# Feed-forward features as rows read back from device memory, prepared one group earlier, and moments as three split products

## The chip, the cores and the metric

The kernel runs on one core of a Trainium2 chip. The time is device microseconds of one execution, and lower is better. The kernel before took 903.79 us (median of 3 runs, 901.78 to 903.89). The engines are PE (matrix products, with its weight loads as PEld), DVE and ACT (elementwise work, reductions, activations), POOL (elementwise work and masks) and SP, which here only issues transfers.

## The reference, cut to what matters

Sixteen sequences of 256 tokens and 256 channels pass four layers, each with a layer norm and a residual sum: attention with 16 heads, a feed-forward layer, a gated linear attention, and the same feed-forward layer again. The change touches the feed-forward layer, whose weights are made from control points by a cubic spline:

```
def spline_reconstruct(control_points, out_size, in_size):
    n = out_size * in_size
    idx, f = _catmull_rom_grid(control_points.shape[0], n)
    p0, p1, p2, p3 = (control_points[idx[0]], control_points[idx[1]], control_points[idx[2]], control_points[idx[3]])
    ...
    return w.reshape(out_size, in_size)
gate_w = spline_reconstruct(gate_cp, INTER, HIDDEN)      # 1024 x 256
up_w = spline_reconstruct(up_cp, INTER, HIDDEN)
down_w = spline_reconstruct(down_cp, HIDDEN, INTER)
gate = jnp.einsum('bsh,ih->bsi', hidden_states, gate_w)
up = jnp.einsum('bsh,ih->bsi', hidden_states, up_w)
inter = jax.nn.silu(gate) * up
return jnp.einsum('bsi,hi->bsh', inter, down_w)
x = x + _L0_ffn_ref(_layernorm(x, axis=-1), ...)
```

## The kernel before

**Stages.** After the weights are set up the program runs attention (one period for each of the 16 sequences), the first feed-forward stage, the gated stage (periods 0 to 16, the last one a tail) and the second feed-forward stage. `X` holds all tokens on the chip from the first stage to the last.

**A feed-forward stage** has 8 groups g of 512 tokens (two sequences), and each group has 8 steps m of 128 of the 1024 inner channels. The rows of the gate and up weights in one step depend on 42 features of a token only: 14 channels of x, 14 further channels half a row on, and 14 moments, which are products of x with a fixed table `mom`. Each feature is needed as a high part, as the rest (low part) and as the high part again, so one step's gate product has 3 x 42 = 126 rows against `cst` (126 x 128). It is one product of 512 columns, and so is the up product. The down product takes the inner values as a high and a low part and is 12 products of 256 columns.

**How the features come about.** DVE normalises four tiles of 128 tokens into `xr` (L1760). PE turns them (L1001), ACT and DVE copy the turned x into `xf`, and PE multiplies it with the moment table (L1012), in 16 products of 128 columns with plain 32-bit operands. ACT and POOL then spread x and moments into `xe` (L1356, L1369, L640 to L648), tokens on the partitions and 126 features for each step on the free axis. In every step PE turns four 128 x 126 pieces of `xe` (L1022) into `bank_t`, and ACT copies them to `stk` (L1374), which has room for two steps.

**Order of the work.** Each engine runs a list written out by hand, group by group in `period` and step by step inside it, and waits on counting semaphores. In step m PE does the turn for step m + 1, the gate and up products of m (L1048, L1051) and the down product of m - 2 (L396 to L398); ACT does `in_hi` of m - 1 (L1387), the copy to `stk` (L1374) and the SiLU of m (L1379); DVE does `in_lo` of m - 1 (L1778) and the gated product `inter` of m (L1773). `gact`, `inter` and `pair_a`/`pair_b` hold two steps, `in_hi`/`in_lo` four. The features of group g + 1 are made during group g, its statistics during group g - 1. SP stores finished groups in the second feed-forward stage and is otherwise idle in both of them. The down weights `wd_lo` are loaded from device memory in 16 transfers near the end of attention (L513), and the attention's `stack` is filled by transfers from `stage` (L484) to 16 partitions each.

Of the kernel before, what the change touches and what calls it, by code (L numbers as in the profile page):

```python
# [20 lines left out]
ALU = mybir.AluOpType  # L21
# [28 lines left out]
XW = 388  # L50
# [96 lines left out]
def build(nc, x, a_wq, a_wk, a_wv, a_wo, b_wq, b_wk, b_wog, b_wig, g_weight, cpw_in, psi_in, feat_in, mom_in,  # L147
          starts, out):
    outer = ExitStack()
    with outer:  # L150
# [22 lines left out]
        half_neg = sb("half_neg", [P, 2, TB], F32)  # L173
# [18 lines left out]
        mom = sb("mom", [P, CT, MT * KG], F32)  # L192

# [13 lines left out]
        with ExitStack() as at:  # L207
            wq, wk, wv = ((sb(n + "_hi", [P, CT, D], F32R, at), sb(n + "_lo", [P, CT, D], F32R, at))
# [9 lines left out]
            stack = sb("stack", [P, 2, 2, PR, 2, S], F32R, at)  # L218
# [12 lines left out]
        with ExitStack() as ft:  # L231
            xr = sb("xr", [P, 2 * TB, XW], F32, ft)
# [36 lines left out]
        wdx = nc.dram_tensor("wdx", [INTER + 1, D], F32, kind="Internal").ap()  # L269

# [3 lines left out]
        s_cp, s_feat, s_mom = sem("control_points_loaded"), sem("features_loaded"), sem("moment_table_loaded")  # L274
        s_c, s_ch = sem("factors_made"), sem("factors_high")
# [49 lines left out]
        def ffn_semaphores():  # L325
# [8 lines left out]
            f.bn, f.mv, f.ve, f.xn, f.xc = own("bn", 4), own("mv", 4), own("ve", 1), own("xn", 4), own("xc", 1)  # L334
            f.up, f.il, f.res = own("up", MT), own("il", MT), own("res", 2)
            f.dve = [f.bn, f.mv, f.ve, f.xn, f.xc, f.up, f.il, f.res]
            f.rs, f.xl, f.ml = own("rs", 1), own("xl", 1), own("ml", 1)
            f.pool = [f.rs, f.xl, f.ml]

            f.xh, f.xa, f.mo, f.mh = own("xh", 1), own("xa", 1), own("mo", 1), own("mh", 1)  # L340
            f.st, f.si, f.ih = own("st", MT), own("si", MT), own("ih", MT)
            f.act = [f.xh, f.xa, f.mo, f.mh, f.st, f.si, f.ih]

            f.xT, f.mp, f.tp = own("xT", 2), own("mp", 1), own("tp", MT)
            f.gp, f.upp, f.dp = own("gp", MT), own("upp", MT), own("dp", MT + 1)
            f.pe = [f.xT, f.mp, f.tp, f.gp, f.upp, f.dp]
# [70 lines left out]
        def run_pairs(period):  # L417

            def run(eng):
                period(0, 0, prev=False)  # L420
                with eng.Fori(0, PAIRS // 2 - 2) as j:
                    period(2 * j + 1, 1)
                    period(2 * j + 2, 0)
                period(PAIRS - 3, 1)
                period(PAIRS - 2, 0, nxt2=False)
                period(PAIRS - 1, 1, nxt=False, nxt2=False)
            return run
# [13 lines left out]

        def gathered(b):

            at = b * (P + 1) + 2
            return xr[:, :, at:at + P].rearrange("p t (m s) -> p t m s", s=KG)[:, :, :, 0:NB]

        def spread(u, copy, b):

            return xe[:, u, :, :, copy, NB * b:NB * b + NB]
# [9 lines left out]
        def _(sp):  # L459
# [9 lines left out]
            lead(sp, a_stk + a_md)  # L469
# [61 lines left out]

            run_periods(sp, period)
            sp.wait_ge(a_res, upto(a_res, B - 1, 1))
# [3 lines left out]
            with sp.Fori(0, PAIRS - 1) as g:  # L537
                sp.wait_ge(f_.res, upto(f_.res, g + PAIRS, 2))
                sp.dma_start(out_t[:, bass.ds(2 * TB * g, 2 * TB), :],
                             X[:, bass.ds(2 * TB * g, 2 * TB), :]).then_inc(s_out, 16)  # L540
# [8 lines left out]
        def _(pool):  # L549
# [6 lines left out]
            pool.memset(half_neg[:, :, :], -0.5).then_inc(s_const, 1)  # L556
# [10 lines left out]
            pool.tensor_copy(ident16[:, :], ident[:, :]).then_inc(s_const, 1)  # L567

            def rstd(b, u):
                pool.wait_ge(a_ve, upto(a_ve, b, 1))  # L570
                pool.tensor_tensor(rs[:, u, :], ve[:, u, :], half_neg[:, 0, :], ALU.pow).then_inc(a_rs, 1)
# [40 lines left out]
            def period(b, j, u, prev=True, nxt=True, nxt2=True, nxt3=True):  # L612
                for p in range(NP):
# [3 lines left out]
                    if nxt and not nxt2:  # L617
# [1341 lines left out]
```

## Time and profile before

| | before |
|---|---|
| median of 3 runs | 903.79 us |
| the profiled execution: its time, its span | 903.31 us, 901.6 us |
| busy: PE, PEld, DVE, ACT, POOL | 829.0, 707.9, 642.2, 541.2, 324.7 us |
| granted TensorE clock, mean | 0.973 |
| first gate product of the first feed-forward stage | 383.37 us |
| first gate product of the second feed-forward stage | 715.08 us |

The profiled execution takes 1.7 us more than its span; that lies outside the first and the last instruction. A busy PE need not be at its peak, since the ends of pipelined products are modelled: what one costs is read from the distance between starts. A granted clock of 1.00 is 2.4 GHz, 0.50 is 1.2 GHz. The DMA share is the mean busy share of 16 transfer engines.

### The profile page before, as it was taken

To read this page: it belongs to the slowest core of one execution; us is meant where nothing else is said; L and a number is where in the kernel's file an instruction comes from. 1 tells how busy PE (TensorE), PEld (TensorE's weight loads), DVE (VectorE), ACT (ScalarE), POOL (GpSimd) and SP (SyncE) were. 2 spreads that over 40 slices of the span, in tenths; PEclk is the share of its full clock that TensorE was granted. 3 is DMA by queue.
4 is the path that set the end of the run, shared out by engine and by line. 5 is a ranking of instruction groups with operands and counts; after the bars stand their busy time and mean duration, and the time that the engine had idled before them with its cause. 6 is when DMAs were issued, how large, how long until landed. Compare 5 with 4: busy or idle time off the path is not lost.

```text
span 901.6 us, 21452 instructions
## 1 busy us (share of the span) xinstructions
PE 829.0 (92%) x7348; PEld 707.9 (79%) x7348; DVE 642.2 (71%) x1287; ACT 541.2 (60%) x1062; POOL 324.7 (36%) x386
## 2 busy tenths in 40 slices
PE   3599899999999997689999999899999799999998
PEld 3477677777777775578888888799998688888887
DVE  7566777777778776457766766688888666667765
ACT  2146445545554554466666667598887566666664
POOL 3932223222322224233323331057666733333320
PEclk9779999999999999799999999999999899999999
DMA  5955666765676562000000000000000000000001
GB/s 178 119 82 85 132 94 97 97 93 83 100 96 88 87 89 49 7 17 1 1 0 0 1 1 1 1 1 0 0 0 1 1 1 25 24 23 23 24 25 47
DMA packets 33767, 40.54 MB, mean 45 GB/s; under 512 B 4335, under 2 KB 25232, under 8 KB 33664
## 3 DMA queue, kind: packets, MB, share of 16 engines
q1 hardware_dynamic: 33706, 39.74, 26.9%
q8 instruction: 36, 0.59, 0.3%
q14 instruction: 25, 0.20, 0.1%
HBM read 8.79 MB, written 5.24 MB: 16 GB/s over the span
## 4 chain that ended last, share of the span: by engine, by line
PE 51%; DVE 16%; ACT 13%; issue 9%; POOL 4%; SPq 3%; DMA 2%; DVEq 1%; ACTq 1%; POOLq 0%
PE bank L396 7%; PE bank L397 6%; PE bank L398 6%; DVE inter L1773 5%; PE pair_a L815 4%; ACT gact L1379 4%; ACT stk L1374 4%; PE bank L829 4%; PE pair_b L784 3%; PE bank L1012 3%; PE pair_b L1138 2%; PE bank L1022 2%; DVE in_lo L1778 2%; DVE st L1747 2%; PE bank L1138 2%
## 5 line engine op out<-in xcount | busy, mean ns | idle before, releaser
L577 POOL TENSOR_SCALAR_AFFINE_SELECT prob<-prob 128x512 f32<-128x512 f32 x128 | 82.3, 643 | 210.0 <-ACT prob L1250 210.0
L396 PE MATMUL bank<-wd_hi,in_hi 128*128 128x256 f32 x512 | 147.7, 288 | 8.5 <-DVE X L1784 6.8
L1778 DVE TENSOR_TENSOR in_lo<-inter,in_hi 128x512 fp32r<-128x512 f32 x128 | 97.7, 763 | 77.9 <-ACT in_hi L1387 77.3
L1250 ACT ACTIVATE prob<-pair_a 128x768 f32<-128x768 f32 x128 | 103.7, 810 | 74.3 <-PE pair_a L815 73.2
L398 PE MATMUL bank<-wd_hi,in_lo 128*128 128x256 f32 x512 | 142.9, 279 | 0.0
L397 PE MATMUL bank<-wd_lo,in_hi 128*128 128x256 f32 x512 | 142.8, 279 | 0.0
L1387 ACT ACTIVATE in_hi<-inter 128x512 fp32r<-128x512 f32 x128 | 80.9, 632 | 94.7 <-DVE inter L1773 94.6
L1618 DVE TENSOR_REDUCE mx<-pair_b 128x6 f32<-128x768 f32 x124 | 118.1, 952 | 26.2 <-PE pair_b L796 25.2
L1773 DVE TENSOR_TENSOR inter<-gact,pair_b 128x512 f32<-128x512 f32 x128 | 87.6, 685 | 36.8 <-ACT gact L1379 36.3
L396 PEld LDWEIGHTS bank<-wd_hi,in_hi 128*128 128x128 f32 x512 | 97.1, 190 | 16.4 <-issue 6.0
L397 PEld LDWEIGHTS bank<-wd_lo,in_hi 128*128 128x128 f32 x512 | 97.5, 190 | 3.6
L398 PEld LDWEIGHTS bank<-wd_hi,in_lo 128*128 128x128 f32 x512 | 96.8, 189 | 0.0
L1022 PE MATMUL bank<-ident,xe 128*126 128x128 f32 x512 | 81.0, 282 | 9.4 <-ACT stk L1374 5.3
L1374 ACT ACTIVATE stk<-bank 126x512 fp32r<-126x512 f32 x128 | 75.2, 587 | 12.8 <-PE bank L1022 12.6
L815 PE MATMUL pair_a<-stack 50*128 50x256 f32 x512 | 66.1, 336 | 14.4 <-DMA stack<-mrow 9.3
L1379 ACT ACTIVATE gact<-pair_a 128x512 f32<-128x512 f32 x128 | 75.9, 593 | 0.0
L1022 PEld LDWEIGHTS bank<-ident,xe 128*126 128x126 f32 x512 | 58.1, 142 | 18.5 <-ACT stk L1374 12.7
L640 POOL COPY xe<-xr 128x448 f32<-128x448 f32 x32 | 24.7, 773 | 130.9 <-ACT xe L1356 130.9
L815 PEld LDWEIGHTS pair_a<-stack 50*128 50x128 f32 x512 | 39.4, 189 | 39.6 <-issue 15.8
L784 PE MATMUL pair_b<-stack 48*128 48x256 f32 x496 | 55.9, 303 | 7.2 <-DVE stage L1609 3.6
L1048 PE MATMUL pair_a<-stk,cst 126*128 126x512 f32 x128 | 62.3, 487 | 0.0
L1238 ACT ACTIVATE stage<-bank 128x512 fp32r<-128x512 f32 x32 | 19.2, 599 | 57.0 <-PE bank L398 52.3
(222 smaller groups left out, 2132.2 us busy)
## 6 DMA issues: line engine op xcount, KB each, us to landing
stack<-stage SPq DMA_DIRECT2D x192, 128.0 KB, 4.7
X<-in_attn_a_x SPq DMA_DIRECT2D x14, 256.0 KB, 5.0
result<-X SPq DMA_DIRECT2D x7, 512.0 KB, 2.9
stack<-mrow SPq DMA_DIRECT2D x128, 4.0 KB
wdx<-spline SPq DMA_DIRECT2D x1, 1024.0 KB
wd_lo<-wdx SPq DMA_DIRECT2D x16, 64.0 KB
spline<-factor_basis SPq DMA_DIRECT2D x1, 1008.0 KB, 6.5
X<-in_attn_a_x SPq DMA_DIRECT2D x1, 512.0 KB, 7.5
```

The source lines that it names most:

```text
L396: pe.matmul(dst, l_hi, r_hi, start=first, stop=False)
L397: pe.matmul(dst, l_hi, r_lo, start=False, stop=False)
L398: return pe.matmul(dst, l_lo, r_hi, start=False, stop=last)
L784: pe.matmul(dst[:, n, at_col:at_col + S], stack[rows, u, h, p % PR, 0, P * t:P * t + P], stack[rows, u, h, p % PR, 1, :], start=(t == 1), ...
L815: i = pe.matmul(pair_a[:, n, at_col:at_col + S], stack[rows, u, h, p % PR, 1, P * t:P * t + P], stack[rows, u, h, p % PR, 0, :], start=Tru ...
L1022: i = pe.transpose(bank_t[0:NFX, P * t:P * t + P], xe[:, u, t, m].rearrange("p c f -> p (c f)").bitcast(F32), ident[:, :])
L1250: act.activation(prob[:, p % 4], pair_a[:, :, P:4 * P], ACT.Exp, scale=DK ** -0.5).then_inc(a_e, 1)
L1374: act.activation(stk[:, m % 2, :], bank_t[0:NFX, :], ACT.Copy).then_inc(f_.st, 1)
L1379: act.activation(gact[:, m % 2, :], pair_a[:, m % 2, :], ACT.Silu).then_inc(f_.si, 1)
L1618: dve.tensor_reduce(mx[:, h, :, p % PR, :], src[:, :, 0:3 * P].rearrange("p n (t k) -> p n t k", t=3), AX.X, ALU.max).then_inc(a_mx, 1)
L1773: dve.tensor_tensor(inter[:, m % 2, :], gact[:, m % 2, :], pair_b[:, m % 2, :], ALU.mult).then_inc(f_.up, 1)
L1778: dve.tensor_tensor(in_lo[:, m % LAG, :], inter[:, m % 2, :], in_hi[:, m % LAG, :].bitcast(F32), ALU.subtract).then_inc(f_.il, 1)
```

## The change

`xe`, its spreading on ACT and POOL, the turns of its pieces on PE and the copies to `stk` are gone. ACT now normalises x into `xr`, PE turns it, ACT and DVE split the turned x into a high part and a low part (`fs`), and PE multiplies both parts with a split moment table in 6 products of 512 columns, whose result ACT and DVE split as well. SP writes `fs` to a table `fx` in device memory, in 3 transfers of 128 x 2 x 512 values, one row for each channel or moment. It then reads back, in 9 transfers of 14 x 8 x 512 values, the 14 rows of each kind for all 8 steps: for the high, the low and the high part again. `stk` holds all 8 steps of two groups. There is one `fx`, so the rows of the next group are written only when the reads of the group before have landed (`f_.ld`), and read only when they have been written (`f_.fw`). Features of group g + 2 are made during group g, their statistics during group g - 1. Features of the first two groups are made at the end of attention and of the gated stage.

On SP, in the loop of a feed-forward stage; `X` is the residual, `result` the output. Before, only the second stage has such a loop:

```order
L539 ISA [waits f_res]
L539 DMA result<-X 128x4x256
L537 REGISTER_ALU
L537 COMPARE_AND_BRANCH
L544 DMA result<-X 128x2x256 [waits f_res] x2
```

Now, for one group in the second stage (the first has the same without `result`):

```order
L555 ISA [waits f_fw]
L561 DMA stk<-fx 14x8x512 [waits f_upp]
L561 DMA stk<-fx 14x8x512 x8
L575 ISA
L576 ISA [waits f_res]
L576 DMA result<-X 128x4x256
L541 ISA
L542 ISA [waits f_xl]
L544 DMA fx<-fs 128x2x512 [waits f_ld]
L544 DMA fx<-fs 128x2x512
L548 REGISTER_ALU
L550 DMA fx<-fs 128x2x512 [waits f_ml]
```

Reads of one group, the store and the writes of the next group take turns, with a wait between reads and writes on either side.

On PE, step 6 of a group before (the 12 down products of a step begin with the last row shown):

```order
L1022 MATMUL bank<-ident,xe 126x128 [waits f_st]
L1022 MATMUL bank<-ident,xe 126x128 x3
L1048 MATMUL pair_a<-stk,cst 128x512 [waits f_si,f_st]
L1051 MATMUL pair_b<-stk,cst 128x512 [waits f_up]
L396 MATMUL bank<-wd_hi,in_hi 128x256 [waits f_il]
```

Now, step 5, the one with the moments of group g + 2 (`fs`, `mom_hi`, `mom_lo`):

```order
L1071 MATMUL pair_a<-stk,cst 128x512 [waits f_si]
L1074 MATMUL pair_b<-stk,cst 128x512 [waits f_up]
L412 MATMUL bank<-fs,mom_hi 128x512 [waits f_xl,moment_table_low]
L413 MATMUL bank<-fs,mom_hi 128x512
L414 MATMUL bank<-fs,mom_lo 128x512
L412 MATMUL bank<-fs,mom_hi 128x512
L413 MATMUL bank<-fs,mom_hi 128x512
L414 MATMUL bank<-fs,mom_lo 128x512
L412 MATMUL bank<-wd_hi,in_hi 128x256 [waits f_il]
```

The turns and the wait for `f_st` are gone from every step. A group's first gate product waits for `f_ld`, its own 9 reads.

The diff, cut (8 leading blanks of each line are left out):

```diff
-XW = 388
+FSTEP = P + 1
+FROWS = 3 * FSTEP + 5
...
-    xf = sb("xf", [P, CT, 2 * S], F32, ft)
-    stk = sb("stk", [NFX, 2, 2 * S], F32R, ft)
-    xe = sb("xe", [P, 2, 2 * TB, MT, 3, NF], F32R, ft)
+    stk = sb("stk", [P, 2, MT, 2 * S], F32R, ft)
+    xr = sb("xr", [P, 2 * TB, D], F32, ft)
+    fs = sb("fs", [P, 2, 3, 2 * S], F32R, ft)
...
+fx = nc.dram_tensor("fx", [2, FROWS, 2 * S], F32, kind="Internal").ap()
...
+        def write_x(g):
+            sp.wait_ge(f_.xl, upto(f_.xl, base + g, CT))
+            sp.wait_ge(f_.ld, upto(f_.ld, base + g - 1, 144))
+            for c in range(CT):
+                sp.dma_start(fx[:, P * c:P * c + P, :].rearrange("v p t -> p v t"),
+                             fs[:, :, c, :].bitcast(F32)).then_inc(f_.fw, 16)
+        def write_moments(g):
+            sp.wait_ge(f_.ml, upto(f_.ml, base + g, 1))
+            at = 2 + 2 * FSTEP
+            sp.dma_start(fx[:, at:at + P, :].rearrange("v p t -> p v t"),
+                         fs[:, :, CT, :].bitcast(F32)).then_inc(f_.fw, 16)
+        def read(g, u):
+            sp.wait_ge(f_.fw, upto(f_.fw, base + g, 48))
+            sp.wait_ge(f_.upp, upto(f_.upp, base + g - 2, MT))
+            for n, part in enumerate((0, 1, 0)):
+                for r in range(3):
+                    rows = fx[part, 2 + FSTEP * r:2 + FSTEP * r + P, :]
+                    rows = rows.rearrange("(m s) t -> s m t", s=KG)[0:NB]
+                    at = NF * n + NB * r
+                    sp.dma_start(stk[at:at + NB, u].bitcast(F32), rows).then_inc(f_.ld, 16)
+        def period(g, u, prev=True, nxt=True, nxt2=True, nxt3=True):
+            if nxt:
+                read(g + 1, 1 - u)
+            if prev:
+                store(g - 1)
+            if nxt2:
+                write_x(g + 2)
+                write_moments(g + 2)
+        return write_x, write_moments, read, run_pairs(period)
...
+    sp.wait_ge(s_zero, 1)
+    sp.dma_start(fx[:, D, :].rearrange("v (p k) -> v p k", k=32), zeros[:, :]).then_inc(s_zeros, 16)
+    f1_write_x(0)
+    f1_write_moments(0)
+    sp.wait_ge(a_stp, upto(a_stp, B - 2, NP))
+    sp.wait_ge(s_zeros, 16)
+    f1_read(0, 0)
+    f1_write_x(1)
+    f1_write_moments(1)
     sp.wait_ge(a_res, upto(a_res, B - 1, 1))
...
                  ).then_inc(s_gload, 16)
     sp.dma_start(win[:, :, :], starts).then_inc(s_gload, 16)
-    with sp.Fori(0, PAIRS - 1) as g:
...
+        def period(g, u, prev=True, nxt=True, nxt2=True, nxt3=True):
+            if nxt3:
+                rstd4(g + 3)
...
-            pe.wait_ge(s_mom, 16)
-            pe.wait_ge(f_.xa, upto(f_.xa, base + g, 1))
-            pe.wait_ge(f_.xc, upto(f_.xc, base + g, 1))
-            for t in range(2 * TB):
-                for c in range(CT):
-                    i = pe.matmul(dst[:, P * t:P * t + P], xf[:, c, P * t:P * t + P], mom[:, c, :],
-                                  start=c == 0, stop=c == CT - 1)
+            pe.wait_ge(s_moml, 1)
+            pe.wait_ge(f_.xl, upto(f_.xl, base + g, CT))
+            for c in range(CT):
+                i = mm3(pe, dst[:, :], mom_hi[:, c, :], mom_lo[:, c, :], fs[:, 0, c, :], fs[:, 1, c, :],
+                        c == 0, c == CT - 1)
             i.then_inc(f_.mp, 1)
-        def turn_rows(g, u, m):
-            pe.wait_ge(f_.st, upto(f_.st, base + g, m))
-            if m == 0:
-                pe.wait_ge(f_.ml, upto(f_.ml, base + g, 1))
-            for t in range(2 * TB):
-                i = pe.transpose(bank_t[0:NFX, P * t:P * t + P],
-                                 xe[:, u, t, m].rearrange("p c f -> p (c f)").bitcast(F32), ident[:, :])
-            i.then_inc(f_.tp, 1)
         def down(g, m):
...
-        def period(g, u, prev=True, nxt=True, nxt2=True):
+        def period(g, u, prev=True, nxt=True, nxt2=True, nxt3=True):
             for m in range(MT):
-                if m < MT - 1:
-                    turn_rows(g, u, m + 1)
-                elif nxt:
-                    turn_rows(g + 1, 1 - u, 0)
-                pe.wait_ge(f_.st, upto(f_.st, base + g, m + 1))
+                if m == 0:
+                    pe.wait_ge(f_.ld, upto(f_.ld, base + g, 144))
                 pe.wait_ge(f_.si, upto(f_.si, base + g, m - 1))
-                pe.matmul(pair_a[:, m % 2, :], cst[:, 0, m, :], stk[:, m % 2, :], start=True,
+                pe.matmul(pair_a[:, m % 2, :], cst[:, 0, m, :], stk[0:NFX, u, m, :], start=True,
                           stop=True).then_inc(f_.gp, 1)
                 pe.wait_ge(f_.up, upto(f_.up, base + g, m - 1))
-                pe.matmul(pair_b[:, m % 2, :], cst[:, 1, m, :], stk[:, m % 2, :], start=True,
+                pe.matmul(pair_b[:, m % 2, :], cst[:, 1, m, :], stk[0:NFX, u, m, :], start=True,
                           stop=True).then_inc(f_.upp, 1)
-                if m in (2, 3) and nxt:
-                    if m == 2:
-                        pe.wait_ge(f_.mh, upto(f_.mh, base + g, 1))
-                    else:
-                        pe.wait_ge(f_.xa, upto(f_.xa, base + g + 1, 1))
-                    turn_in(g + 1, 1 - u, m - 2, bank_p)
-                if m == 4 and nxt:
-                    moments(g + 1, bank_p)
+                if m == 2 and nxt2:
+                    pe.wait_ge(f_.ml, upto(f_.ml, base + g + 1, 1))
+                    turn_in(g + 2, 0, bank_t)
...
+        def normalise4(g):
+            act.wait_ge(f_.mr, upto(f_.mr, base + g, 1))
+            act.wait_ge(f_.xT, upto(f_.xT, base + g - 1, CT))
+            act.sem_inc(passed_act, 1)
+            for t in range(2 * TB):
+                act.activation(xr[:, t, :], X[:, bass.ds(2 * TB * g + t, 1), :], ACT.Identity,
+                               bias=fnmr[:, t:t + 1], scale=frs[:, t:t + 1]).then_inc(f_.xn, 1)
+        def high_x(g, c, src):
+            act.wait_ge(f_.xT, upto(f_.xT, base + g, c + 1))
+            act.wait_ge(f_.fw, upto(f_.fw, base + g - 1, 48))
+            act.activation(fs[:, 0, c, :], src[:, :], ACT.Copy).then_inc(f_.xh, 1)
+        def high_moments(g, src):
             act.wait_ge(f_.mp, upto(f_.mp, base + g, 1))
-            act.activation(xr[:, :, D + 4:XW], src[:, :].rearrange("p (t k) -> p t k", t=2 * TB),
...
                     high_inner(g if m else g - 1, (m - 1) % MT)
-                if m < MT - 1:
-                    rows(g, m + 1)
-                elif nxt:
-                    rows(g + 1, 0)
                 silu(g, m)
-                if nxt:
+                if nxt2:
+                    if m == 0:
+                        normalise4(g + 2)
                     if m == 2:
-                        high_x(g + 1, 1 - u)
-                        store_turned(g + 1, bank_p)
-                    if m == 4:
-                        high_moments(g + 1, 1 - u, bank_p)
+                        high_x(g + 2, 0, bank_t)
+                        high_x(g + 2, 1, bank_p)
+                    if m == 5:
+                        high_moments(g + 2, bank_t)
...
+        def low_x(g, c, src):
+            dve.wait_ge(f_.xh, upto(f_.xh, base + g, c + 1))
+            dve.tensor_tensor(fs[:, 1, c, :], src[:, :], fs[:, 0, c, :].bitcast(F32),
+                              ALU.subtract).then_inc(f_.xl, 1)
+        def low_moments(g, src):
+            dve.wait_ge(f_.mh, upto(f_.mh, base + g, 1))
+            dve.tensor_tensor(fs[:, 1, CT, :], src[:, :], fs[:, 0, CT, :].bitcast(F32),
+                              ALU.subtract).then_inc(f_.ml, 1)
...
-                    stats4(g + 2)
-                if m == 3 and nxt:
-                    store_turned(g + 1, bank_p)
+                if nxt3:
+                    if m < 2:
+                        stats2(g + 3, m)
+                    if m == 1:
+                        mean_rest(g + 3)
+                if nxt2:
+                    if m == 2:
+                        low_x(g + 2, 0, bank_t)
+                    if m == 3:
+                        low_x(g + 2, 1, bank_p)
+                    if m == 5:
...
                 g_products(n)
             if nxt:
                 g_values(n + 1, 1 - u)
+            if at == B - 3:
+                pe.wait_ge(g_.xl, upto(g_.xl, B - 1, 1))
+                f2_turn(0, 0, bank_t)
+            if at == B - 2:
+                f2_moments(0, bank_t)
             if not prev:
                 g_turn(n + 2, u)
```

## Rows read from the trace of the kernel before

**Rows 1.** Windows view, one stretch of the first feed-forward stage; its columns are the first row.

```profile
core 0: us, PE busy (x) PEld busy (x) DVE busy (x) ACT busy (x) POOL busy (x), PEclk, DMA share, GB/s
430.00:453.00 23.00, 22.40 (x171) 20.14 (x170) 16.19 (x33) 15.19 (x29) 7.13 (x7) 1.00 0.01 1
```

**Rows 2.** Timeline of PE: start, us, engine, line, operation, output<-inputs, count, [idle<-releaser].

```profile
452.67 0.47 PE L1048 MATMUL pair_a<-stk,cst 126*128 126x512 f32 x1
...
454.47 0.28 PE L398 MATMUL bank<-wd_hi,in_lo 128*128 128x256 f32 x1
454.75 0.65 PE L1022 MATMUL bank<-ident,xe 128*126 128x128 f32 x4
455.17 0.48 PE L1048 MATMUL pair_a<-stk,cst 126*128 126x512 f32 x1
...
464.91 2.02 PE L1012 MATMUL bank<-mom,xf 128*128 128x128 f32 x16 [0.21 <-DVE xf L1767]
466.69 0.36 PE L396 MATMUL bank<-wd_hi,in_hi 128*128 128x256 f32 x1
```

**Rows 3.** Timeline of ACT in the same stretch.

```profile
453.58 0.63 ACT L1387 ACTIVATE in_hi<-inter 128x512 fp32r<-128x512 f32 x1 [0.89 <-DVE inter L1773]
454.12 0.58 ACT L1374 ACTIVATE stk<-bank 126x512 fp32r<-126x512 f32 x1
454.60 0.59 ACT L1379 ACTIVATE gact<-pair_a 128x512 f32<-128x512 f32 x1
```

**Rows 4.** Timeline of DVE in the same stretch.

```profile
455.38 0.69 DVE L1773 TENSOR_TENSOR inter<-gact,pair_b 128x512 f32<-128x512 f32 x1 [0.43 <-ACT gact L1379]
...
458.48 1.28 DVE L1784 TENSOR_TENSOR X<-bank,X 128x512 f32 x2
...
470.61 1.40 DVE L1747 BATCH_NORM_STATS2 st<-X 128x6 f32 x4
...
472.58 0.17 DVE L1754 TENSOR_SCALAR ve<-mv 128x4 f32<-128x4 f32 x1
```

**Rows 5.** Timeline of PE: first gate products of both stages' first and last group.

```profile
383.37 0.47 PE L1048 MATMUL pair_a<-stk,cst 126*128 126x512 f32 x1
...
545.87 0.48 PE L1048 MATMUL pair_a<-stk,cst 126*128 126x512 f32 x1
...
715.08 0.77 PE L1048 MATMUL pair_a<-stk,cst 126*128 126x512 f32 x1
...
876.11 0.48 PE L1048 MATMUL pair_a<-stk,cst 126*128 126x512 f32 x1
```

**Rows 6.** Timeline of SP's queue, then windows view, while `wd_lo` is loaded.

```profile
349.63 6.04 SPq L513 DMA_DIRECT2D wd_lo<-wdx  x16
356.00:357.00 1.00, 0.84 (x17) 0.47 (x17) 0.00 (x0) 1.00 (x2) 0.23 (x2) 1.00 0.59 88
```

**Rows 7.** Windows view, stack loads queued.

```profile
28.00:30.00 2.00, 0.00 (x0) 0.00 (x0) 0.00 (x0) 0.39 (x1) 1.83 (x2) 1.00 1.06 118
```

**Rows 8.** The page's DMA issues (us to landing), and windows view of one store.

```profile
result<-X SPq DMA_DIRECT2D x7, 512.0 KB, 2.9
770.50:771.00 0.50, 0.50 (x3) 0.10 (x1) 0.00 (x0) 0.50 (x2) 0.34 (x1) 1.00 1.02 346
```

**Rows 9.** One line of the program (L534, load of `gw_row`): its landing.

```profile
DMA to landing us min/median/max: 3.0/3.0/3.0
```

**Rows 10.** Timeline of PE and windows view behind an idle stretch.

```profile
363.92 0.80 PE L815 MATMUL pair_a<-stack 50*128 50x256 f32 x4 [4.78 <-DMA stack<-mrow]
364.00:366.00 2.00, 2.00 (x20) 1.01 (x20) 1.65 (x5) 1.57 (x3) 0.28 (x1) 0.50 0.01 4
```

**Rows 11.** Timeline of ACT in the last attention period.

```profile
363.21 0.63 ACT L1298 ACTIVATE wd_hi<-wd_lo 128x512 fp32r<-128x512 f32 x1 [3.88 <-DMA wd_lo<-wdx]
```

**Rows 12.** Timeline of PE at the end of the gated stage.

```profile
699.05 2.75 PE L1138 MATMUL pair_b<-val,spline 128*128 128x256 f32 x12
...
712.71 0.91 PE L1022 MATMUL bank<-ident,xe 128*126 128x128 f32 x4 [3.11 <-POOL xe L648]
```

More of the change, by code:

```diff
@@ L1071, in run @@
                     down(PAIRS - 1, MT - 1)
-                return turn_in, moments, turn_rows, run
+                return turn_in, moments, run
             def g_turn(n, u, dst=bank_t):
@@ L1321, in period @@
                         spread_rows(2 * p + 1)
+                    if isinstance(b, int) and b == 1 and p == 4:
+                        act.wait_ge(s_mom, 16)
+                        act.activation(mom_hi[:, :, :], mom[:, :, :], ACT.Copy).then_inc(s_momh, 1)
+                    if nxt and not nxt2 and p == 7:
+                        f1_normalise(0)
                     if not nxt:
-                        if p == 0:
-                            act.wait_ge(s_gc, 1)
-                            f1_high_x(0, 0)
+                        if p in (1, 5):
+                            for c in range(CT):
+                                f1_high_x(p // 4, c, pair_b[:, c, :])
                         if p == 2:
-                            f1_store_turned(0, pair_b[:, 0, :])
-                        if p in (3, 4, 5, 7):
-                            high_down(min(p - 3, 3))
-                        if p == 6:
-                            f1_high_moments(0, 0, pair_b[:, 0, :])
+                            f1_normalise(1)
+                        if p in (3, 7):
+                            f1_high_moments(p // 4, pair_b[:, 0, :])
+                        if p in (2, 4, 6, 7):
+                            high_down((p - 1) // 2)
                     if p == 0:
@@ L1411, in run @@
                     high_inner(PAIRS - 1, MT - 1)
-                return high_x, store_turned, high_moments, rows, run
+                return normalise4, high_x, high_moments, run
             def g_high_turned(n, u, src=bank_t):
@@ L1499, in period @@
                         g_normalise(n - 2, u)
-                    if cur and not nxt:
-                        f2_high_x(0, 0)
-                        f2_store_turned(0, bank_t)
-                    if not cur:
-                        f2_high_moments(0, 0, bank_t)
+                    at = n if isinstance(n, int) else None
+                    if at == B - 2:
+                        f2_high_x(0, 0, bank_t)
+                    if at == B - 1:
+                        f2_high_moments(0, bank_t)
+                        f2_normalise(1)
+                    if at == B:
+                        f2_high_x(1, 1, bank_p)
                     if nxt2 and prev:
                         g_norm(n + 2, u)
+                    if at == B - 3:
+                        f2_normalise(0)
                     if prev:
@@ L1548, in _ @@
             copy_att(B - 1)
-            f1_rows(0, 0)
             run_f1()
```

310 lines of the change are left out of this document (156 added, 154 removed).

## The prediction

> **What bounds the kernel now.** I read the windows view first, one group of a feed-forward stage. PE is busy for 22.40 of 23.00 us at a granted clock of 1.00, DVE for 16.19, ACT for 15.19, POOL for 7.13, and the transfers move 1 GB/s [rows 1]. So these stages wait for PE, and the transfer engines stand idle. The distance between first and last group gives the period: (545.87 - 383.37) / 7 = 23.2 us in the first stage, (876.11 - 715.08) / 7 = 23.0 in the second [rows 5]. Inside a group the timeline of PE comes next. A step without moments takes 455.17 - 452.67 = 2.50 us. Its last down product starts at 454.47 and the turns at 454.75. A product of 256 columns takes about 0.12 at full clock, so PE stands for about 0.16 us before the turns, and the turns take 455.17 - 454.75 = 0.42 [rows 2]. Behind PE runs a loop of ACT and DVE that is nearly as long as the step: `in_hi`, the copy to `stk`, SiLU (0.59), then the gated product on DVE (0.69), which releases the next `in_hi` [rows 3, 4].
>
> **What goes.** PE loses 8 x (0.42 + 0.16) = 4.6 us a group. That leaves 1.92 us for a step (the gate product at 452.67 to the last down product's end), 8 x 1.92 = 15.4 for a group. The turns of x stay: two of 0.42 and about 0.2 of waits, 1.0. The moments took 466.69 - 464.91 = 1.78 us in 16 products [rows 2]; 6 products of 512 columns at some 0.23 (twice the 0.12) are 1.4. PE then needs 15.4 + 1.0 + 1.4 = 17.8 us. ACT loses the copy to `stk`, 454.60 - 454.12 = 0.48 us, out of the loop, which falls from 2.50 to about 2.02, 8 x 2.02 = 16.2 us [rows 3]. POOL's spreading lies beside other work and goes at no gain, but for the wait of 3.11 us before the second stage [rows 12].
>
> **What comes on ACT and DVE.** DVE's statistics are cut in two halves in steps 0 and 1. In step 1 stand half of four statistics, the operations on means (0.17 each, four or five of them) and the residual sum of two products at 1.28 [rows 4]: 0.7 + 0.7 + 1.3 = 2.7 us beside the gated product and `in_lo`, which leave some 0.9 of a step free. That costs about 1.8 us a group, between 0 (if the two-step buffers catch it) and 2.7. Normalising on ACT adds four tiles, of which I take 0.5 us onto the loop, and the bound is 0 to 1.6. The feature work ends there: 16.2 + 1.8 + 0.5, with the wait at the moments, is 19.3 us where PE needs 17.8. If nothing else bound the group, it would lose 3.8 us.
>
> **What comes on SP, and takes the bound.** There is one `fx`, and its writes and reads exclude each other. Reads of g + 1 wait for its three writes; writes of g + 2 wait for those nine reads. A group starts when its reads have landed. So a group can't be shorter than T = R + W, reads plus writes with their latencies, whatever the engines do.
> W: three writes of 512 KB. Such a store has landed 2.9 us after its issue, and the transfers move 346 GB/s meanwhile [rows 8]. The two others add 524 KB / 346 = 1.5 each: W = 2.9 + 3.0 = 5.9 us.
> R: 9 transfers of 14 x 8 x 2 KB are 2.064 MB. The fixed part comes from a load of 128 KB that lands after 3.0 us [rows 9]: less its own transfer it is some 1.6 us, or up to 2.6. The rate of loads to 14 partitions isn't in the trace. Near rows are loads to 8 partitions at 88 GB/s on a share of 0.59 of 16 engines, 9.3 GB/s for a busy engine (11 if only 8 carried them) [rows 6]; loads to 16 partitions from on-chip memory at 118 GB/s, 7.4 an engine [rows 7]; and stores at 346 GB/s, 21.6 an engine [rows 8]. If 14 engines serve 14 partitions, these make 130, 154, 103 and 303 GB/s. I take 132, the loads from device memory by their share: 15.7 us, R = 17.3, with ends at 8.4 (303 GB/s) and 21.6 (103).
> T = 17.3 + 5.9 = 23.2 us: by chance the period of before. PE would be idle for T - 17.8, some 5 us at each group's start.
>
> The Trainium skill has a rule for such transfers ("SBUF — State Buffer", section "Door 1: The DMA port swizzle"): the bandwidth goes by how many of 16 ports the partitions reach, four partitions in a row share one, and four ports give about 109 GB/s. Fourteen partitions in a row reach four. The trace is a little above it for 16 partitions (118) and well above it for 8, where two ports would be 54 GB/s and the row shows 88 [rows 6, 7]; I go by the rows from device memory. By the page's figure the sum would be some 966 us, an estimate. That is close to the third rival, which the rows give by themselves.
>
> **The clock.** Behind an idle stretch of 4.78 us PE runs at a granted clock of 0.50 for the next two microseconds at least [rows 10]; a gate product then takes 0.77 in place of 0.48 [rows 5]. With PE idle for 5 us in every group, several microseconds run at 0.50 in each: 17.8 + 4 = 22 us from the group's start, the end of the group's work. It still fits in 23.2, as the reads don't wait for it.
>
> **The sum**, against the profiled execution of 903.31 us (0.5 below the median):
> Entry of the first stage: in the last attention period ACT waits for `wd_lo` until 363.21 [rows 11], and the split of group 0's moments stands behind that. Three us of work and 2.9 of landing make 369.2; + 17.3 = 386.5 for the first gate product, against 383.37 [rows 5]: +3.1.
> Seven periods: 7 x (23.2 - 23.2) = 0. The last group has no reads behind it and runs at compute's pace, -3.8, but starts after idle at half clock, +3; with the wait for its reads I take +1.5 in all, bounds -3 and +4.
> Entry of the second stage: group 0's moments come in period 14 of the gated stage, behind the products at 699.05 [rows 12]. They are split and written at about 705.9; + 17.3 = 723.2 against 715.08: +8.1. The 3.11 us of POOL's wait are gone but inside this.
> Seven periods: 7 x (23.2 - 23.0) = +1.4. Stores of 512 KB share the engines with the reads, six at 0.3, +1.8. Last group: +1.
> Sum: 3.1 + 0 + 1.5 + 8.1 + 1.4 + 1.8 + 1 = +16.9, so **920 us**. R stands in it 16 times (14 periods, two entries): each microsecond of R is 16 us of time. The forecast is no change where R is 16.2, or 141 GB/s. A fixed part between 1.2 and 2.8 us puts the case at 905 to 944.
>
> **Rivals.** *Reads at 11 GB/s an engine (not slower).* For it: the share of 0.59 counts waits in the queue as busy, and 8 engines would carry 8 partitions. 154 GB/s gives R = 13.4 + 1.6 = 15.0, T = 20.9, 2.3 less, 16 x 2.3 = 37 off the forecast: 883 us. It decides from 141 GB/s up. Against it: idle PE for 3 us in each group, whose half clock comes back as compute that lasts as long as T.
> *The engines set the pace.* If the rate goes by engine as in stores, T is 14.3 and the engines' 19.3 bounds: 7 x (19.3 - 23.2) + 7 x (19.3 - 23.0) = -53, entries and ends -1: 849 us. This is what the change does if transfers are hidden; it needs 178 GB/s or more. For it: 21.6 GB/s is what one engine has been seen to carry [rows 8]. Against it: no row of a load to few partitions comes near.
> *Reads like the stack's.* 103 GB/s gives R = 21.6, T = 27.5, 16 x 4.3 = 69 more: 989 us. For it: the same size of tile, the same count of partitions. Against it: those loads also read from on-chip memory.
> *The two effects cancel* by chance, within 0.3% (900.6 to 906.0), about what a measurement of this kernel can tell from no change.
>
> **Chances.** Forecast (905 to 944) 0.37, 11 GB/s an engine 0.25, engines set the pace 0.14, like the stack 0.18, the rest between them 0.06. Faster by over 0.3%: 0.25 + 0.14 + 0.02 = 0.41; within: 0.04; slower: 0.37 + 0.18 = 0.55. The range takes in all of the second, nearly all of the third and the lower part of the fourth (by 16 us for each of R, up to R = 20.5): 848 to 972.
>
> **What would show it.** In the trace after: each group's first gate product idle for about 5 us with the transfer to `stk` as its releaser; first gates 23.2 us apart, and not 19.3, 20.9 or 27.5; the nine reads landing some 17 us behind the first one's issue and the writes within 6; mean traffic of (2.06 + 1.57 MB) / 23.2 us = 157 GB/s; first gates at about 386.5 and 723; a granted clock of 0.50 at group starts; a step of ACT and DVE of about 2.0 us without `stk`. The prediction is wrong if first gates don't wait for transfers at all (R below 13.4), or if the reads move at another rate than 132 GB/s; the period then tells which. It is wrong too if steps of PE stay at 2.5 us, since then the turns weren't what a step costs.

## The result, and the profile after

The changed kernel takes 969.96 us (median of 4 runs, 962.88 to 972.51), the kernel before 903.15 us (with a fourth run beside the three listed above): a ratio of 1.0729, with an interval of 1.0666 to 1.0793, slower. The forecast was 920. The profiled execution has a span of 970.5 us, 68.9 more than before. Medians here leave out a slow execution, one over 1.5% above the fastest of the same kernel; there is one, among the ten of e2.

The page of the kernel after: a summary by engine, the group of the gate product (busy us, mean ns | idle us before it and what ended it), the chain of what ended last, and two DMA issues.

```profile
span 970.5 us, 19870 instructions
PE 803.6 (83%) x6676; PEld 684.8 (71%) x6676; DVE 632.1 (65%) x1272; ACT 502.4 (52%) x967; POOL 237.2 (24%) x306
...
PE 41%; DMA 37%; SPq 9%; DVE 5%; issue 3%; POOL 3%; ACT 3%; ACTq 0%; POOLq 0%; DVEq 0%
...
L1071 PE MATMUL pair_a<-stk,cst 126*128 126x512 f32 x128 | 59.9, 468 | 102.1 <-DMA stk<-fx 102.1
...
fx<-fs SPq DMA_DIRECT2D x48, 512.0 KB, 4.0
...
result<-X SPq DMA_DIRECT2D x7, 512.0 KB, 17.0
```

PE works 25 us less than before and is idle 102.1 us in front of the first gate product of a group, each time until `stk<-fx` has landed. DMA has 37% of the chain, where it had 2%.

Gate products that end such a wait, in the timeline of PE of the kernel after (the first, second and last group of the first stage, and of the second):

```profile
396.28 0.77 PE L1071 MATMUL pair_a<-stk,cst 126*128 126x512 f32 x1 [6.13 <-DMA stk<-fx]
421.32 0.79 PE L1071 MATMUL pair_a<-stk,cst 126*128 126x512 f32 x1 [5.88 <-DMA stk<-fx]
...
581.00 0.79 PE L1071 MATMUL pair_a<-stk,cst 126*128 126x512 f32 x1 [10.03 <-DMA stk<-fx]
...
764.92 0.77 PE L1071 MATMUL pair_a<-stk,cst 126*128 126x512 f32 x1 [7.28 <-DMA stk<-fx]
790.07 0.49 PE L1071 MATMUL pair_a<-stk,cst 126*128 126x512 f32 x1 [3.57 <-DMA stk<-fx]
...
945.89 0.79 PE L1071 MATMUL pair_a<-stk,cst 126*128 126x512 f32 x1 [8.67 <-DMA stk<-fx]
```

The period is (581.00 - 396.28) / 7 = 26.4 us, and (945.89 - 764.92) / 7 = 25.9 in the second stage. Before it was 22.9 and 23.0, and not 23.2 and 23.0 as the prediction had it. The row at 545.87 in [rows 5] isn't the first gate product of the last group but its second: a stage has 64 gate products, eight for each group, and the 57th starts at 543.58. Timeline of PE before:

```profile
543.58 0.48 PE L1048 MATMUL pair_a<-stk,cst 126*128 126x512 f32 x1
545.87 0.48 PE L1048 MATMUL pair_a<-stk,cst 126*128 126x512 f32 x1
```

So the period before is (543.58 - 383.37) / 7 = 22.9 us. SP's queue in the kernel after shows what the period is made of. A row is a run of issues with its start and its length.

```profile
474.27 0.89 SPq L544 DMA_DIRECT2D fx<-fs  x2
475.32 0.77 SPq L550 DMA_DIRECT2D fx<-fs  x1
479.94 3.83 SPq L561 DMA_DIRECT2D stk<-fx  x9
500.62 0.90 SPq L544 DMA_DIRECT2D fx<-fs  x2
501.64 0.81 SPq L550 DMA_DIRECT2D fx<-fs  x1
506.28 3.82 SPq L561 DMA_DIRECT2D stk<-fx  x9
527.24 0.90 SPq L544 DMA_DIRECT2D fx<-fs  x2
```

Writes are issued as soon as the reads have landed, and the next reads as soon as the writes have: W = 479.94 - 474.27 = 5.7 and 506.28 - 500.62 = 5.7 us, R = 500.62 - 479.94 = 20.7 and 527.24 - 506.28 = 21.0. Over the seven groups of the stage R is 20.1 on the mean (18.0 to 21.1) and W 6.3 (5.7 to 7.4). The windows view of the kernel after, inside the reads of another group (columns as in [rows 1]):

```profile
457.00:465.00 8.00, 8.00 (x58) 7.48 (x57) 6.51 (x10) 4.54 (x9) 0.00 (x0) 1.00 0.94 112
432.00:440.00 8.00, 8.00 (x58) 7.47 (x56) 6.47 (x10) 4.46 (x8) 0.00 (x0) 1.00 0.94 129
```

The transfer engines are busy for 0.94 of the time and move only 112 GB/s. The second row is inside the reads of the group before, the shortest ones of the stage (R = 446.50 - 428.52 = 18.0): there the same transfers ran at 129. So 112 is the usual rate and not a fixed one; nothing here shows why that group's was higher.

### The profile page after: what moved, and what is told of

Its sections match the earlier page's. It is cut to its first block, busy times and chain, and to the rows that moved or that the text cites. A ratio compares the mean times of both kernels' runs of the same rounds, so it can differ in the third digit from the quotient of the medians.

```text
span 970.5 us, 19870 instructions
## 1 busy us (share of the span) xinstructions
PE 803.6 (83%) x6676; PEld 684.8 (71%) x6676; DVE 632.1 (65%) x1272; ACT 502.4 (52%) x967; POOL 237.2 (24%) x306
## 2 busy tenths in 40 slices
DMA packets 64997, 98.67 MB, mean 102 GB/s; under 512 B 7153, under 2 KB 28050, under 8 KB 64898
## 4 chain that ended last, share of the span: by engine, by line
PE 41%; DMA 37%; SPq 9%; DVE 5%; issue 3%; POOL 3%; ACT 3%; ACTq 0%; POOLq 0%; DVEq 0%
DMA stk<-fx 27%; DMA fx<-fs 8%; PE bank L412 6%; SPq L561 5%; PE bank L413 4%; PE bank L414 4%; PE pair_a L850 4%; PE bank L864 3%; PE pair_b L819 3%; PE pair_b L1159 2%; PE bank L1159 2%; PE pair_a L1124 1%; POOL spline L649 1%; PE pair_b L831 1%; PE bank L868 1%
## 5 line engine op out<-in xcount | busy, mean ns | idle before, releaser
L413 PE MATMUL bank<-wd_lo,in_hi 128*128 128x256 f32 x512 | 153.7, 300 | 0.0
L414 PE MATMUL bank<-wd_hi,in_lo 128*128 128x256 f32 x512 | 153.7, 300 | 0.0
L1071 PE MATMUL pair_a<-stk,cst 126*128 126x512 f32 x128 | 59.9, 468 | 102.1 <-DMA stk<-fx 102.1
L1825 DVE TENSOR_TENSOR in_lo<-inter,in_hi 128x512 fp32r<-128x512 f32 x128 | 89.0, 696 | 63.4 <-ACT in_hi L1415 62.6
L412 PEld LDWEIGHTS bank<-wd_hi,in_hi 128*128 128x128 f32 x512 | 107.5, 210 | 18.1 <-DVE X L1831 6.0
L413 PEld LDWEIGHTS bank<-wd_lo,in_hi 128*128 128x128 f32 x512 | 106.9, 209 | 5.7
L414 PEld LDWEIGHTS bank<-wd_hi,in_lo 128*128 128x128 f32 x512 | 106.4, 208 | 0.0
L1071 PEld LDWEIGHTS pair_a<-stk,cst 126*128 126x128 f32 x128 | 27.9, 218 | 106.1 <-issue 63.4
L689 POOL TENSOR_TENSOR frs<-fve,half_neg 128x4 f32<-128x4 f32 x16 | 17.2, 1076 | 209.5 <-DVE fve L1799 209.5
L1074 PE MATMUL pair_b<-stk,cst 126*128 126x512 f32 x128 | 57.0, 445 | 0.0
L819 PEld LDWEIGHTS pair_b<-stack 48*128 48x128 f32 x496 | 40.0, 194 | 14.3 <-DVE mx L1653 7.6
L1268 ACT ACTIVATE stage<-bank 128x512 fp32r<-128x512 f32 x32 | 19.1, 597 | 56.8 <-PE bank L414 52.0
```

Source lines behind the costliest of these rows:

```text
L412: pe.matmul(dst, l_hi, r_hi, start=first, stop=False)
L413: pe.matmul(dst, l_hi, r_lo, start=False, stop=False)
L414: return pe.matmul(dst, l_lo, r_hi, start=False, stop=last)
L819: pe.matmul(dst[:, n, at_col:at_col + S], stack[rows, u, h, p % PR, 0, P * t:P * t + P], stack[rows, u, h, p % PR, 1, :], start=(t == 1), ...
L1071: pe.matmul(pair_a[:, m % 2, :], cst[:, 0, m, :], stk[0:NFX, u, m, :], start=True, stop=True).then_inc(f_.gp, 1)
L1825: dve.tensor_tensor(in_lo[:, m % LAG, :], inter[:, m % 2, :], in_hi[:, m % LAG, :].bitcast(F32), ALU.subtract).then_inc(f_.il, 1)
```

## The experiments

My theory after the result (P): the rate of 112 GB/s is set by where the rows land, 14 neighbouring partitions of the on-chip memory. The rival (Q): it is the price of a 2 KB packet from device memory on each transfer engine. Beside it stood three more questions: whether the chain of reads and writes really holds the group, what pace the engines keep without it, and what mutual exclusion costs.

**e1: rows 9 partitions apart.** The read and the order of factor rows to match it:

```diff
-at = NF * n + NB * r
-sp.dma_start(stk[at:at + NB, u].bitcast(F32), rows).then_inc(f_.ld, 16)
+at = 3 * n + r
+sp.dma_start(stk[at:at + 9 * NB - 8:9, u].bitcast(F32), rows).then_inc(f_.ld, 16)
-cx = sb("cx", [P, 2, MT, 3, NF], F32R, at)
+cx = sb("cx", [P, 2, MT, NB, 9], F32R, at)
```

Expected: 

> The changed kernel with one thing different: the 14 rows of a read land on partitions 9 apart (0, 9, ... 117 and so on) in place of 14 neighbours, and the factors' rows are stored in the same new order, so the product is the same. Bytes, packets, transfers and engines used are the same. Theory P (the rate is set by how far the 14 partitions of one transfer lie apart): reads go from 112 to some 200 to 300 GB/s, R from 20 to 9-12 us, the engines' 19.3 us bounds a group, total 850 to 870 us. Theory Q (each engine takes some 270 ns for a 2 KB packet from device memory, wherever it lands): R stays 20 us, groups 26.1 us, total 965 to 975 us.

Measured: 862.92 us (862.04 to 864.62), a ratio to the kernel before of 0.9547 (0.9514 to 0.958), and 107 us below the changed kernel. SP's queue, the windows view inside reads, and PE's timeline in e1:

```profile
406.74 7.46 SPq L561 DMA_DIRECT2D stk<-fx  x9
417.78 0.88 SPq L544 DMA_DIRECT2D fx<-fs  x2
```

```profile
409.00:415.00 6.00, 3.72 (x29) 3.35 (x28) 5.06 (x15) 2.94 (x6) 1.21 (x2) 0.97 0.77 252
```

```profile
455.89 0.39 PE L412 MATMUL bank<-wd_hi,in_hi 128*128 128x256 f32 x1 [2.12 <-DVE X L1837]
```

Same bytes, packets (64997 in the whole trace, as in the changed kernel) and rows in device memory: R is at most 417.78 - 406.74 = 11.0 us and the rate 252 GB/s (227 to 245 in windows of 8 us inside the reads of five groups). Q falls. No gate product waits for `stk<-fx` now; the one long wait left in a group is for DVE's residual sum.

**e2 and e3: fewer bytes.** From the third group of a stage on, three of nine reads (e2) or all nine (e3) bring one step of eight:

```diff
+first = isinstance(g, int) and g < 2
+steps = 1 if n in (2,) and not first else MT      # e3: n in (0, 1, 2)
-rows = rows.rearrange("(m s) t -> s m t", s=KG)[0:NB]
+rows = rows.rearrange("(m s) t -> s m t", s=KG)[0:NB, 0:steps]
```

Expected of e2: 

> The changed kernel, but from the third group of each stage on the three reads of the second high copy bring only the first of eight steps (the other steps keep older values, so this part of the computation is left out). Bytes of a group's reads fall from 2.06 to 1.46 MB. Chain theory (a group lasts reads plus writes): at 112 GB/s R is 13.0 + 1.6 = 14.6, a group 20.3 us, 12 groups lose 5.8 each, 70 in all: 900 us. Rival (something else holds the group at 26, the reads only end beside it): within 10 us of 970.

Expected of e3: 

> As before, with all nine reads cut to one of eight steps from the third group of each stage on (the values of the other steps are old ones): reads are then 0.26 MB a group. The transfer chain would be some 11 us a group, so this shows the pace of the engines alone. My estimate of 19.3 us gives 12 x 6.8 = 82 less, 888 us. Rival: the engines' own pace is worse than worked out (DVE crowd, normalising on ACT, moments), 21 to 22 us: 908 to 920 us. If it is PE alone (17.8): 870.

Measured: 908.46 us (901.97 to 914.01) and 887.51 us (880.9 to 889.03). The last gates of the first stage in both (PE timeline, e2 first):

```profile
525.51 0.50 PE L1073 MATMUL pair_a<-stk,cst 126*128 126x512 f32 x1 [1.61 <-DMA stk<-fx]
546.58 0.80 PE L1073 MATMUL pair_a<-stk,cst 126*128 126x512 f32 x1 [5.01 <-DMA stk<-fx]
```

```profile
424.06 0.79 PE L1073 MATMUL pair_a<-stk,cst 126*128 126x512 f32 x1 [6.20 <-DMA stk<-fx]
```

In e2 the wait for `stk<-fx` stands in front of every short group of the stage but one, and their period is 20.7 us (5 periods; 21.1 in the second stage), where the chain was worked out at 20.3: with three tenths less to read it still ends last. The total is 8 us above the 900 expected, and far from the rival's 960 to 980. In e3 the row shown is the last such wait of that stage, the second group's; from the third on no gate product waits, and groups follow each other at 19.0 and 19.2 us (5 periods of either stage). So 19.1 us is the engines' own pace on the mean, where I had worked out 19.3. Part of that agreement is luck: the last two of the five periods have no statistics in them, and the last one no features either (18.2 and 15.6 to 16.0 us), which the 19.3 didn't allow for. The three full ones take 19.7 to 21.4 us, 20.5 on the mean.

**e4: two tables.** Writes of a group wait for the reads of the last but one:

```diff
-fx = nc.dram_tensor("fx", [2, FROWS, 2 * S], ...)
+fx = nc.dram_tensor("fx", [2, 2, FROWS, 2 * S], ...)
-sp.wait_ge(f_.ld, upto(f_.ld, base + g - 1, 144))
+sp.wait_ge(f_.ld[v], upto(f_.ld[v], base + g - 2, 144 - 72 * v))
```

Expected: 

> The changed kernel with two tables in device memory, one for even and one for odd groups, so that the writes of a group no longer wait for the reads of the group before; all is still issued by SP in the same order. Chain theory: the writes stand behind the reads in the queue and the next reads wait for the writes, so that only the latency between reads and writes goes, some 1.5 to 2 us a group: 24.3 us a group, 942 to 950 us. Rival (mutual exclusion is what costs, transfers of both kinds would overlap): the group falls to the reads alone, 20 us, total 885 us.

Measured: 951.53 us (948.6 to 955.3). SP's queue in e4:

```profile
495.21 3.83 SPq L561 DMA_DIRECT2D stk<-fx  x9
503.40 0.90 SPq L544 DMA_DIRECT2D fx<-fs  x2
507.56 0.36 SPq L550 DMA_DIRECT2D fx<-fs  x1
520.35 3.82 SPq L561 DMA_DIRECT2D stk<-fx  x9
```

The writes are issued 8.2 us after the reads, in the middle of them, but the next reads start no earlier than 25.1 us after the last ones, for the bytes queue. The mean period is 24.3 us in the first stage, as expected; the total is just above the 942 to 950, and far from the rival's 885. Exclusion costs the latency between the two, some 2 us a group; the bytes cost the rest.

**e5 and e6: other spacings.** Eight of nine reads with a step of 2 and of 8 partitions, one execution each (the factors keep their old order, so rows and factors don't match; the time is what is read):

```diff
+k = 3 * n + r
+at = k // d * d * NB + k % d                 # d = 2 in e5, 8 in e6; the ninth read at 112, d = 1
+sp.dma_start(stk[at:at + d * NB - d + 1:d, u].bitcast(F32), rows)...
```

Expected of e5: 

> The changed kernel with the 14 rows of a read on every second partition (28 partitions across) in eight of the nine reads; the ninth keeps neighbours. The factors keep their old order, so the products mix wrong features; the time is what counts. Theory P in its general form (the rate grows with how many partitions the rows are spread over, linearly): 28 partitions give twice 112, 224 GB/s. By the ports that the Trainium skill lists (SBUF - State Buffer, Door 1) 14 rows on every second partition reach 7 ports, 190 GB/s. Rival: only far spacing helps, 112 stays. I expect the fast reads to bring R down to 12 to 13 us, the group to the engines' pace of 19.9 to 21.3, total 865 to 885 us.

Expected of e6: 

> As before with rows on every eighth partition (105 across) in eight of the nine reads. If the span of partitions counts, this is as fast as spacing 9 (R 11 us, where SP's issuing at 0.85 us each is the bound). By the ports that the skill lists, 14 rows on every eighth partition reach 8 ports only (spacing 9 reaches 14): 218 GB/s, slightly better than spacing 2. The 8 fast reads would then last 1.84 MB / 218 = 8.4 us and the ninth 2.0 at 112. Total 860 to 875 us in both cases; the rows of DMA traffic tell them apart.

Measured: 892.58 and 884.08 us. Windows view inside reads, e5 and then e6:

```profile
469.00:475.00 6.00, 6.00 (x43) 5.56 (x42) 4.58 (x8) 3.97 (x7) 0.00 (x0) 1.00 0.93 184
```

```profile
463.50:469.00 5.50, 5.50 (x40) 5.14 (x39) 4.56 (x8) 2.71 (x5) 0.00 (x0) 1.00 0.92 194
```

Both totals are above what I expected (by 8 and 9 us at the nearer end), since groups still waited for reads now and then. The rates are what decides: 112, 184, 194 and 252 GB/s at a step of 1, 2, 8 and 9. From 2 to 8 the rows spread over nearly four times as many partitions and the rate hardly rises; from 8 to 9 they spread over 118 in place of 105, and it jumps. So P in the form "the wider the faster" falls too; it is which partitions, not how far. The step from 184 to 194 is small beside what one window can tell: over ten microseconds of reads the rate is 186 to 189 in three groups of e5 and 188 to 192 in four of e6. R is 14.9 us on the mean of five groups in e5 and 14.3 in e6.

The Trainium skill ("SBUF — State Buffer", section "Door 1: The DMA port swizzle") gives the partitions of 16 ports, by which the rows reach 4, 7, 8 and 14 ports, and as estimates from its figure of four ports 109, 190, 218 and 381 GB/s. The runs agree at 7 ports and, in the window at 112, at 4 (the group at 129 is above it); they are 11% below at 8 and show a part of the rise at 14. By the same table the port with most of a read's 14 rows has 4, 2, 2 and 1 of them. That count would make e5 and e6 alike, as they nearly are; it wasn't tested apart from the number of ports. At 14 ports SP's issuing comes near to being the limit: its nine issues take 7.46 us, and 2.064 MB in that time are 277 GB/s; the share of the transfer engines is only 0.77. That it is the limit wasn't tested.

**e7: statistics away from the residual sum.** In e1 PE waits 1.9 to 2.3 us for L1837 in groups 1 to 4 of each stage, during which statistics are made, and 0.3 to 0.6 us in groups 5 and 6, where none are. e7 is e1 with:

```diff
-if m < 2:
-    stats2(g + 3, m)
-if m == 1:
-    mean_rest(g + 3)
+if m in (0, 4):
+    stats2(g + 3, m // 4)
+if m == 6:
+    mean_rest(g + 3)
```

Expected: 

> The kernel with spaced partitions (e1) and the second half of DVE's statistics moved from step 1 to step 4, the operations on means from step 1 to step 6, away from the residual sum. In e1 PE waits 2.12 us for the residual sum in each group. Crowd theory (the statistics in step 1 push the residual sum back): the wait goes to 0 to 0.4, and the group from 19.9 to 21.3 falls to 18 to 19; 14 groups by 1.7 to 2.3 are 24 to 32 us, and 862.9 becomes 830 to 840. Rival (the loop of ACT and DVE is the bound anyway, 16.2 us and its side work): under 8 us of gain, 855 to 863.

Measured: 844.57 us (841.2 to 844.91), 0.9317 of the kernel before (0.9283 to 0.935). PE's timeline and the windows view of a group in e7:

```profile
449.71 0.39 PE L412 MATMUL bank<-wd_hi,in_hi 128*128 128x256 f32 x1 [0.45 <-DVE X L1837]
```

```profile
405.85:424.00 18.15, 17.79 (x127) 16.54 (x127) 15.30 (x32) 12.42 (x24) 1.21 (x2) 1.00 0.62 220
```

The wait falls from 2.12 to 0.45 us and the group to 18.2 us, nearly all of it PE's work. The gain, 18.4 us, is under the 24 to 32 expected, which put the wait into 14 groups: it stands in eight, and e1's groups lasted 19.5 us on the mean and not 19.9 to 21.3. Crowding is shown, its price over the whole was overstated.

**e8: e7 with two tables.** Expected: 

> e7 with the two tables of e4. With spaced partitions reads and writes together last some 17 us. If a group of e7 is at 18 or above, the transfers are hidden and two tables change nothing: within 3 us of e7. If e7's groups have fallen to where the transfer chain ends last, the tables give back up to 1.8 us for each of them, 25 us at most.

Measured: 845.67 us (845.31 to 850.03), 1.1 us from e7. The transfers are hidden there, and exclusion costs nothing.

**e9 and e10: a loss far from the change.** The attention stage ran some 5 us longer in the first trace of the changed kernel. Expected of e9, the changed kernel again: 

> The changed kernel once more, to look at 66 to 90 us, in attention, which the change doesn't touch. There the first trace has a granted clock of 0.50 from 74 to 83 us and loses some 5 us to the kernel before. If that is a property of this kernel, the dip is there again; if it is chance of an execution, it may be gone, and the total is then some 5 us below 970, as the fastest run of the changed kernel (962.88).

Expected of e10, e1 again: 

> The kernel with spaced partitions (e1) once more, for the same look: its first trace has no dip there. If the dip is chance, it may show one here, and the total is then some 5 us above 863.

Measured: 968.43 and 863.06 us. Windows view of 74 to 83 us in the first trace of the changed kernel, in e9, in e1 and in e10:

```profile
74.00:83.00 9.00, 9.00 (x57) 7.73 (x60) 2.10 (x4) 6.13 (x16) 0.65 (x2) 0.50 0.60 73
```

```profile
74.00:83.00 9.00, 9.00 (x60) 7.74 (x62) 2.23 (x4) 6.13 (x16) 0.77 (x2) 0.50 0.59 72
```

```profile
74.00:83.00 9.00, 8.83 (x101) 7.53 (x100) 4.99 (x10) 7.13 (x18) 1.92 (x3) 1.00 0.62 77
```

```profile
74.00:83.00 9.00, 8.83 (x100) 7.53 (x100) 4.29 (x9) 7.13 (x18) 1.97 (x4) 1.00 0.72 88
```

The changed kernel has a granted clock of 0.50 there both times, with 57 and 60 products where e1 has 101 and 100. Of the seven traces with the factors in the old order (the changed kernel twice, e2 to e6) five have such a stretch, e6 a shorter one, and e5 none; of the four in the new order (e1, e7, e8, e10) none has, and the kernel before, with the old order, has none either. So it is more than the chance of one execution, but what tips the clock isn't settled: e5 runs the same attention stage as the changed kernel and keeps 1.00.

## Why the prediction was wrong

The direction and the mechanism were right: reads and writes of one table take turns, T = R + W binds the group, and PE idles in front of every first gate. The direction had a chance of only 0.55 and hung on the value taken for one rate, so little was claimed with it. The step that failed is the term "The rate of loads to 14 partitions isn't in the trace ... I take 132". It was about 112, and R 20.1 us in place of 17.3; R stands in the sum 16 times. The measured 970 lies inside the stated range by 2 us, at an end that was set by R up to 20.5 and not by a forecast.

Step by step, in microseconds of the span, forecast and then measured:

| part | forecast | measured |
|---|---|---|
| attention, up to its last periods | 0 | +6.6 |
| entry of the first stage, beyond that | +3.1 | +6.3 |
| seven periods, first stage | 0 | +24.5 |
| last group of the first stage | +1.5 | -1.0 |
| gated stage | 0 | +4.2 |
| entry of the second stage | +8.1 | +9.2 |
| seven periods and stores, second stage | +3.2 | +19.9 |
| last group | +1 | -0.9 |
| sum | +16.9 | +68.8 |

- **Rate.** The two stages' periods are 44.4 us of the 68.8 and were forecast at 3.2; that miss of 41 is four fifths of the whole. In the first stage it is R by 2.8 us a group and W by 0.4 (6.3 for 5.9), 7 x 3.2 = 22, and another 2 from the period before, which was 22.9 and not the 23.2 taken from the wrong row. The fixed part of R was right: 2.064 MB at 112 GB/s are 18.4, and 1.7 are left for it, where I had 1.6. I had turned the rows into a rate for a busy engine and scaled by 14 engines. The changed kernel, e5, e6 and e1 move the same packets at 112, 184, 194 and 252 GB/s, so a rate for an engine is not a thing to carry over. The nearest row by shape, 16 partitions at 118 GB/s [rows 7], was the right one, and I set it aside because its source was on-chip memory. The rule of the Trainium skill ("SBUF — State Buffer", section "Door 1: The DMA port swizzle") that the prediction weighed and set aside gives 109 GB/s, within 3% of the 112. That its sum of some 966 us is so near 970 is in part luck, since the 10.8 us of attention and the gated stage are in none of its terms. Why the loads to 8 partitions, which I held against it, ran above that rule at 88 GB/s [rows 6] was not tested.
- **Slips in the sum.** With the period before at 22.9 the forecast would have been 922. The row it scales gives 130 GB/s for 14 engines and not 132, worth 2 us. R at 109 GB/s is 18.9 + 1.6 = 20.5, so the sum by that rate is 971 and not 966. A fixed part of 1.2 to 2.8 us gives 914 to 939, not 905 to 944. None comes near the size of what R was off by.
- **The third rival** (reads like the stack's, 989 us) had the nearest rate, 103 GB/s. The real one lies between it and the forecast, nearer to it.
- **Attention.** +6.6 was in no term (SP's last but one issue of maxima rows is at 337.58 before and 344.20 after). Of it 1.7 are there at the stack loads that start at 60.19 before and 61.86 after, from no cause that I can name; the clock at 74 to 83 us goes with the other 5.
- **Entries.** In the first, group 0's moments were written and the reads issued at 376.47, which is 369.9 without attention's delay, where I had 369.2; the first gate product came 19.8 us later. In the second the reads were issued 744.14 - 739.70 = 4.4 us behind the products of period 14, not 6.9; the first gate product came 20.8 us later, which took more than that back.
- **Gated stage.** The feature work in its last periods was left out. Timeline of PE, before and after, the last three periods up to the products of period 14 (before: 672.84 to 699.05 in [rows 12], 26.2 us; after: 30.2, of which PE is busy for 2.4 more, 27.77 in place of 25.34):

```profile
672.84 2.75 PE L1138 MATMUL bank<-val,spline 128*128 128x256 f32 x12
```

```profile
709.49 2.75 PE L1159 MATMUL bank<-val,spline 128*128 128x256 f32 x12
...
739.70 2.75 PE L1159 MATMUL pair_b<-val,spline 128*128 128x256 f32 x12
```

- **The terms of PE held, the loop behind it less so.** A step of PE without moments was worked out at 1.92 us and the moments at 1.4. PE's timeline of the kernel after:

```profile
455.98 0.39 PE L1071 MATMUL pair_a<-stk,cst 126*128 126x512 f32 x1
...
457.87 0.39 PE L1071 MATMUL pair_a<-stk,cst 126*128 126x512 f32 x1
...
460.21 0.40 PE L412 MATMUL bank<-fs,mom_hi 128*128 128x512 f32 x1
...
461.61 0.28 PE L412 MATMUL bank<-wd_hi,in_hi 128*128 128x256 f32 x1
```

The step is 1.89, the moments 1.40, and a group of e7 has 17.79 us of PE against 17.8. The crowd on DVE was put at 1.8 us a group and costs 1.9 to 2.3 in e1, in four groups of each stage. A full group of e3 takes 20.5 us and not 19.3, so that part of the engines' pace was 1.2 us too low. The engines' gain is real: 2.4 us in a full group of e3, some 3.7 on the mean of the last five periods (22.8 to 19.1), and e1 and e7 end 40 and 59 us below 903.15.
- **Half clock** at group starts was there (0.79 us for a gate product, where 0.48 is the usual one) and fitted beside the reads, as worked out.

## What to carry to other kernels

Here the rate of a load went by which on-chip partitions its rows reach: in reads of 14 rows the same bytes took 20.1 us on neighbours and at most 11.0 spaced by 9. When nothing in a trace has the shape of the new transfer, take the row with the same count and place of partitions, not a rate for an engine. If on-chip rows may stand in any order (here the rows of a contraction, with the factors in the same order), spacing them is nearly free: here it cost SP some 3.6 us more of issuing for nine reads, off the path that binds. When transfers fill a buffer in turns, write the group's floor as reads plus writes, and ask what each microsecond of it is multiplied by before choosing a value for a rate.

## What was not expected of the hardware

Spacing by 8 partitions (194 GB/s) is worse than spacing by 9 (252), though nearly as wide, and hardly better than spacing by 2 (184). SP's issue of a read took 0.43 us to neighbours (nine in 3.83) and 0.83 spaced by 9 (nine in 7.46), about the same at a step of 2 (7.24), so it goes with the spacing and not with the rate, and at 9 comes near to being the limit. The same reads to neighbours ran at 129 GB/s in one group and at 112 in the next, for no cause shown. And the changed kernel lost 5 us at a granted clock of 0.50 in a stage whose code the change leaves alone, in both of its traces.
